# Expert sums split in two: thirteen blocks summed and stored while the last seven run, the last seven added to the output by accumulating DMAs

## What is computed

```python
x = hidden_states.reshape(-1, D)                      # 1024 tokens x 256
router_logits = x @ w_gate.T                          # 8 experts
routing_weights = softmax(router_logits)
routing_weights, selected_experts = top_k(routing_weights, 2)
routing_weights = routing_weights / sum(routing_weights)
out = zeros_like(x)
for e in range(8):
    expert_weight = sum(routing_weights * (selected_experts == e), axis=-1)
    h = silu(x @ w1[e].T) * (x @ w3[e].T)             # 704 wide
    out = out + h @ w2[e].T * expert_weight
x = x + out
```

## Time and profile before

| | |
|---|---|
| median of three runs | 648.27 us |
| the profiled execution's own time | 646.59 us |
| its span, first to last instruction | 644.8 us |
| PE busy | 506.1 us, 78% of the span |
| DVE busy | 420.6 us, 65% |
| ACT busy | 367.4 us, 57% |
| POOL busy | 150.1 us, 23% |
| first gather of the expert stage | 461.63 us |
| last result copied by ACT | 627.84 us |
| first load of `ypair` issued | 630.54 us |
| last store to `out` issued | 641.37 us |

### The profile page before, as it was taken

The page is one execution under the profiler, slowest core; times in us unless marked ns, Lnnn a source line. Parts: engine busy times, 40 slices in busy tenths (PEclk is TensorE's granted clock), DMA queues, the critical chain, the costliest instruction groups (busy, mean ns, idle before and its releaser), DMA issues.

```text
span 644.8 us, 14042 instructions
## 1 busy us (share of the span) xinstructions
PE 506.1 (78%) x5716; PEld 371.9 (58%) x5716; DVE 420.6 (65%) x632; ACT 367.4 (57%) x793; POOL 150.1 (23%) x115
## 2 busy tenths in 40 slices
PE   0287788786778855579979999986399999999980
PEld 0154555564556722354655665676399999995560
DVE  7989999999995578979986677668411111111214
ACT  7996899887888227648578657672312222221212
POOL 1000000000020228602229766410202222222110
PEclk9995699897977989799999999996699999999995
DMA  8700000000010000000000000001699999888816
GB/s 332 231 1 1 1 2 1 2 1 1 2 34 2 1 1 1 1 1 2 2 3 4 3 2 3 4 4 34 206 420 418 420 390 326 330 326 326 340 39 204
DMA packets 18336, 71.19 MB, mean 110 GB/s; under 512 B 4832, under 2 KB 9696, under 8 KB 14688
## 3 DMA queue, kind: packets, MB, share of 16 engines
q1 hardware_dynamic: 15120, 64.00, 26.2%
q0 software_dynamic: 1920, 5.25, 2.2%
q10 hardware_dynamic: 1232, 1.06, 0.5%
HBM read 65.57 MB, written 4.72 MB: 109 GB/s over the span
## 4 chain that ended last, share of the span: by engine, by line
PE 44%; DVE 40%; ACT 8%; issue 4%; DMA 2%; POOL 1%; DVEq 0%; POOLq 0%; ACTq 0%
PE PS L1522 29%; DVE arena L975 5%; DVE arena L968 4%; DVE nmx L1071 4%; DVE arena L1236 4%; PE PS L2055 2%; PE PS L1857 2%; PE PS L2124 2%; PE PS L1874 1%; DVE R L997 1%; DVE arena L990 1%; DVE arena L995 1%; DVE arena L994 1%; DVE arena L989 1%; DVE arena L987 1%
## 5 line engine op out<-in xcount | busy, mean ns | idle before, releaser
L1522 PE MATMUL PS<-arena 128*128 128x128 f32 (+5 forms) x1360 | 147.2, 286 | 16.6 <-DVE arena L1171 11.5
L1522 PEld LDWEIGHTS PS<-arena 128*128 128x128 f32 (+3 forms) x1360 | 122.8, 163 | 40.4 <-issue 23.7
L622 ACT ACTIVATE arena<-PS,nmx 128x128 f32<-128x128 f32 (+1 forms) x128 | 52.4, 433 | 21.6 <-DVE nmx L1071 21.5
L1470 DVE TENSOR_TENSOR R<-arena,PS 128x128 f32<-128x128 f32 x16 | 4.6, 288 | 89.0 <-ACT arena L885 89.0
L1587 PE MATMUL PS<-arena 32*128 32x128 f32 (+1 forms) x128 | 23.0, 440 | 32.3 <-ACT arena L622 32.3
L489 POOL DMA_INDIRECT ypair<-arena,oid x20 | 19.8, 988 | 122.3 <-ACT arena L891 122.3
L393 POOL TENSOR_SCALAR arena<-ident,gcol 128x128 f32<-128x128 f32 x4 | 3.7, 934 | 185.3 <-DMA gcol<-in_gcol 185.3
L1522 PE MATMUL PS<-arena,R 128*128 128x256 f32 x192 | 44.2, 380 | 0.6 <-ACT arena L891 0.6
L455 POOL TENSOR_TENSOR arena<-arena 128x1024 f32<-128x1024 f32 x16 | 37.6, 2372 | 21.6 <-DVE arena L1284 21.6
L1522 PEld LDWEIGHTS PS<-arena,R 128*128 128x128 f32 x192 | 35.2, 190 | 5.1 <-issue 1.0
L975 DVE TENSOR_TENSOR_SCAN arena<-dmat,arena 128x1023 f32<-128x1023 f32 x16 | 37.6, 2348 | 0.6
(11 more groups left out here) (319 smaller groups left out, 1170.2 us busy)
## 6 DMA issues: line engine op xcount, KB each, us to landing
arena<-in_moe SPq DMA_DIRECT2D x23, 1408.0 KB, 7.1
arena<-in_moe SPq DMA_DIRECT2D x23, 768.0 KB, 9.2
inproj<-in_inproj SPq DMA_DIRECT2D x1, 1344.0 KB, 10.5
arena<-in_fT SPq DMA_DIRECT2D x2, 512.0 KB, 4.2
R<-in_w1T SPq DMA_DIRECT2D x1, 1024.0 KB, 6.7
R<-in_w2T SPq DMA_DIRECT2D x1, 1024.0 KB, 8.7
R<-in_w3T SPq DMA_DIRECT2D x1, 1024.0 KB, 10.7
xT<-in_xT SPq DMA_DIRECT2D x1, 1024.0 KB, 12.7
```

The lines of the kernel that those rows point to most:

```text
L622: sc.activation(pr[u % 2][:, j, 0:n], PS[:, 2 * (u % 2) + j // 2, (j % 2) * 256:(j % 2) * 256 + n], ACT.Exp, bias=nmx[:, u % 2, j:j + 1], ...
L1522: last = mm(dst, l, r, start=(n == 0), stop=(n == len(pairs) - 1))
```

## The change

The order of the blocks becomes 0 to 8 (whole), 16, 17, 18 (two), 19 (one), 9 to 15 (whole). So the last LATE = 7 steps, 13 to 19, are whole blocks, in each of which a token occurs at most once.

- The rows of steps 0 to 12 go to `ypair` as before. SP then loads all of `ypair` (eight loads of 256 KB, all on SP's queue), behind its last load of weights. DVE sums them into `xtok`, two multiply-adds per row tile, in the middle of its work on the late steps: three quarters after `hidden_block(15)`, the last after `hidden_block(16)`. SP stores each quarter to `out`.
- Rows of `ypair` that only late steps would write must be zero. So SP fills the 2048 rows from a zero tile at the start, and also 896 new rows behind the 1024 of `out`, where padding rows of late steps go. The caller takes the first 1024 rows of the output tensor.
- In steps 13 to 19 ACT multiplies the rows by their weights as it copies them out of PSUM. These weights lie by token, not by row of a block. So `wt` is stored to a new DRAM table `wtab` (after SP's sixth set of weights), and POOL gathers one float per partition for each late block, in the turns of steps 3 to 9.
- POOL adds each late block's rows to `out` by an indirect DMA that accumulates (`compute_op=ALU.add`). Each waits for the block's result, for all four stores to `out`, and for the accumulating DMA before it. POOL's gathers for steps 17 to 19 are issued ahead of the first of these.
- DVE computes the indices of the weights and of the output rows (`late_rows`, eight instructions of 128x7) before its first hidden block.
- ACT's four loads and eight multiplications of the tail and DVE's four additions go.

```diff
-STEPS = [("whole", b) for b in range(15)] + [("two", 16), ("two", 17), ("two", 18), ("one", 19), ("whole", 15)]
+STEPS = [("whole", b) for b in range(9)] + [("two", 16), ("two", 17), ("two", 18), ("one", 19)] + [("whole", b) for b in range(9, 16)]
+LATE = 7
+LATE_OF = slice(16 - LATE, 16)
...
+            sp.wait_ge(S["pool_made"], 1)
+            load(ypair[0:OUT, :].rearrange("(i p) n -> p i n", p=P), zero[:].unsqueeze(1).broadcast_to([P, OUT // P, D]), "route")
+            load(out[N:N + LATE * P, :].rearrange("(i p) n -> p i n", p=P), zero[:].unsqueeze(1).broadcast_to([P, LATE, D]), "route")
...
-
-            sp.wait_ge(st_y, 16 * BLK)
+                if n == RING - 1:
+                    sp.wait_ge(S["act_xtok"], 3)
+                    sp.dma_start(wtab.rearrange("(p w) n -> p (w n)", p=P), wt[:].rearrange("p s i -> p (s i)")).then_inc(st_row, 16)
+
+            sp.wait_ge(st_y, 16 * (BLK - LATE))
             for q in range(4):
-                sp.dma_start(y01[:, 0, 2 * q:2 * q + 2, :], rows_of(0, q)).then_inc(ld_y[q], 16)
+                for s in range(2):
+                    sp.dma_start(y01[:, s, 2 * q:2 * q + 2, :], rows_of(s, q)).then_inc(ld_y[q], 16)
             for i in range(0, NT, 2):
                 sp.wait_ge(S["dve_out"], i // 2 + 1)
                 sp.dma_start(out[P * i:P * (i + 2), :].rearrange("(i p) n -> p i n", p=P), xtok[:, i:i + 2, :])\
                     .then_inc(st_out, 16)
             sp.wait_ge(st_out, 16 * NT // 2)
+            sp.wait_ge(st_y, 16 * BLK)
...
-            for s in range(BLK):
+            pool.wait_ge(ld["route"], 9 * 16)
+            for s in range(BLK - LATE):
                 b = STEPS[s][1]
                 pool.wait_ge(S["act_y"], s + 1)
                 pool.indirect_dma_start(ypair, bass.IndirectOffsetOnAxis(ap=oid[:, b:b + 1], axis=0),
                                         yb[s % YB], None).then_inc(st_y, 16)
                 if s + XR < BLK:
                     gather(s + XR)
+                if 3 <= s < 3 + LATE:
+                    l = s - 3
+                    pool.wait_ge(st_row, 48)
+                    pool.wait_ge(S["dve_gid"], 2)
+                    pool.indirect_dma_start(wlate[:, l:l + 1], None, wtab,
+                                            bass.IndirectOffsetOnAxis(ap=wid[:, l:l + 1], axis=0)).then_inc(ld_w, 16)
+            for s in range(BLK - LATE, BLK - XR):
+                gather(s + XR)
+            for l in range(LATE):
+                s = BLK - LATE + l
+                pool.wait_ge(S["act_y"], s + 1)
+                pool.wait_ge(S["dve_gid"], 3)
+                pool.wait_ge(st_out, 16 * (NT // 2))
+                pool.wait_ge(st_y, 16 * s)
+                pool.indirect_dma_start(out, bass.IndirectOffsetOnAxis(ap=addid[:, l:l + 1], axis=0),
+                                        yb[s % YB], None, compute_op=ALU.add).then_inc(st_y, 16)
...
-                sc.activation(yb[b % YB], bank(7, 256), ACT.Copy).then_inc(S["act_y"], 1)
+                if b < BLK - LATE:
+                    sc.activation(yb[b % YB], bank(7, 256), ACT.Copy).then_inc(S["act_y"], 1)
+                else:
+                    l = b - BLK + LATE
+                    act.wait_ge(ld_w, 16 * LATE)
+                    sc.activation(yb[b % YB], bank(7, 256), ACT.Copy, scale=wlate[:, l:l + 1]).then_inc(S["act_y"], 1)
...
-            act.wait_ge(st_y, 16 * BLK)
-            for q in range(4):
-                act.dma_start(y01[:, 1, 2 * q:2 * q + 2, :], rows_of(1, q)).then_inc(ld_y[q], 16)
-            for i in range(NT):
-                if i % 2 == 0:
-                    act.wait_ge(ld_y[i // 2], 32)
-                sc.activation(yw[:, i, :], y01[:, 1, i, :], ACT.Copy, scale=wt[:, 1, i:i + 1]).then_inc(S["act_yw"], 1)
...
+            def early_sums(q):
+
+                dve.wait_ge(ld_y[q], 32)
+                for i in (2 * q, 2 * q + 1):
+                    for s in range(2):
+                        done(v.scalar_tensor_tensor(xtok[:, i, :], y01[:, s, i, :], wt[:, s, i:i + 1], xtok[:, i, :], ALU.mult, ALU.add),
+                             "dve_out" if i % 2 and s else "dve_self")
...
+            late_rows()
             for s in range(BLK):
                 if s and STEPS[s - 1][0] != "whole":
                     turned_hidden(s - 1)
                 hidden_block(s)
+                if s == BLK - LATE + 2:
+                    dve.wait_ge(S["act_xtok"], 3)
+                    for q in range(3):
+                        early_sums(q)
+                if s == BLK - LATE + 3:
+                    early_sums(3)
```

More of the change, by code:

```diff
@@ L49, with build @@
 MAGIC = 1.5 * 2.0 ** 23
-def build(nc, a, arow, ypair, out):
+def build(nc, a, arow, ypair, wtab, out):
     F = mybir.dt.float32
@@ L240, in build @@
         tokv = spent_gate[:, 512:512 + NT * 2 * NU].bitcast(BF).rearrange("p (s i h v b) -> p s i h v b", s=2, i=NT, h=2, v=2)
-        y01 = arena[:, 0:2 * NT * D].rearrange("p (s i n) -> p s i n", s=2, i=NT)
-        yw = arena[:, 2 * NT * D:3 * NT * D].rearrange("p (i n) -> p i n", i=NT)
+        y01 = R[:, 2:4].rearrange("p s c n -> p s (c n)").rearrange("p s (i n) -> p s i n", i=NT)
         uiota = sb("uiota", [P, NU])
@@ L277, in build @@
         gid = sb("gid", [P, BLK], U32)
+        zero = arena[:, 26 * K + 512:26 * K + 768]
+        addid, addreal, wid, wpart = (sb(n, [P, LATE], U32) for n in ("addid", "addreal", "wid", "wpart"))
+        over = sb("over", [P, LATE])
+        wlate = sb("wlate", [P, LATE])
         PS = ctx.enter_context(nc.psum_tensor("PS", [P, 8, HALF], F))
@@ L292, in build @@
         st_y = sem("st_y")
+        ld_w = sem("ld_w")
         st_out = sem("st_out")
@@ L300, in build @@
             pe_y act_y dve_tokv pe_ids dve_gid dve_out pe_up pe_w act_w dve_xdt dve_xw pe_s act_s act_xbd pe_t
-            act_hgt act_rs dve_dec act_decay dve_rinv pe_r act_rT dve_num act_ekq act_ekvq act_sq act_yw
+            act_hgt act_rs dve_dec act_decay dve_rinv pe_r act_rT dve_num act_ekq act_ekvq act_sq
             dve_hqt dve_iden dve_msq dve_peak pe_rows pe_ss pool_made pool_osc pool_root dve_ht pe_ht""".split()
@@ L383, in _ @@
             done = chained(pool, "pool_self")
+            done(pool.memset(zero[:], 0.0))
             pool.memset(vv[:, :, :, HD:VW], 0.0).then_inc(S["pool_made"], 1)
@@ L695, in out_rows @@
                     act.wait_ge(S["pe_ot"], i - 1)
+                else:
+                    act.wait_ge(ld["route"], 9 * 16)
                 sc.activation(otok[i % 2], bank(4, D), ACT.Copy, scale=oscale3[:, i:i + 1])\
@@ L1382, in places @@
                 h = slice(lo, hi)
-                dve.wait_ge(ld["route"], 7 * 16)
+                dve.wait_ge(ld["route"], 9 * 16)
                 dve.wait_ge(S["pe_rank"], 4 if lo else 1)
@@ L1497, in turned_hidden, with late_rows @@
                     done(v.tensor_copy(h[0:64, 640:640 + UNIT], PS[0:64, u, 5 * UNIT:6 * UNIT]), "dve_ht")
+            def late_rows():
+                rows_ = oid[:, LATE_OF]
+                done(v.tensor_scalar(wpart[:], rows_, P - 1, None, ALU.bitwise_and))
+                done(v.tensor_scalar(wid[:], rows_, 7, None, ALU.logical_shift_right))
+                done(v.tensor_scalar(wid[:], wid[:], 2 * NT - 1, None, ALU.bitwise_and))
+                done(v.scalar_tensor_tensor(wid[:], wpart[:], float(2 * NT), wid[:], ALU.mult, ALU.add), "dve_gid")
+                done(v.tensor_scalar(over[:], rows_, float(N), -float(N), ALU.is_ge, ALU.mult))
+                done(v.tensor_tensor(addreal[:], rows_, over[:], ALU.add))
+                done(v.tensor_scalar(over[:], rows_, float(OUT), -float(P * LATE_OF.start), ALU.is_ge, ALU.mult))
+                done(v.tensor_tensor(addid[:], addreal[:], over[:], ALU.add), "dve_gid")
+            def early_sums(q):
[4 more added lines that the diff above has]
+                             "dve_out" if i % 2 and s else "dve_self")
             for h in hb:
                 done(v.memset(h[64:128, 640:768], 0.0))
+            late_rows()
             for s in range(BLK):
@@ L2237, in program @@
             for n, v in arrays.items()}
-    out = nc.dram_tensor("out_0", (N, D), mybir.dt.float32, kind="ExternalOutput").ap()
+    out = nc.dram_tensor("out_0", (N + LATE * P, D), mybir.dt.float32, kind="ExternalOutput").ap()
     arow = nc.dram_tensor("arow", (N, D), mybir.dt.float32, kind="Internal").ap()
     ypair = nc.dram_tensor("ypair", (OUT + BLK * P, D), mybir.dt.float32, kind="Internal").ap()
-    build(nc, args, arow, ypair, out)
+    wtab = nc.dram_tensor("wtab", (P * 2 * NT, 1), mybir.dt.float32, kind="Internal").ap()
+    build(nc, args, arow, ypair, wtab, out)
 def kernel(**inputs):
@@ L2253 @@
     got = r.results[0]["out_0"]
-    return np.ascontiguousarray(got).reshape(B, T, D)
+    return np.ascontiguousarray(got[0:N]).reshape(B, T, D)
```

## The result

The changed kernel takes 655.21 us (median of 4 runs, 654.69 to 655.7) against 648.12 of the kernel before, a ratio of 1.0101 with a 95% interval of 1.0077 to 1.0125. It is slower by about 7 us. Forecast were 643.6, with 638.6 to 651.0 as the range.

A forecast was written before the change was run, and what follows sets the result against it. Bound by TensorE's steps plus a 17.0 us tail behind the last result. Chain start 616.6 plus seven links, 23.1, gives 639.7; plus 0.4, span 640.1 against 644.8, 4.7 less; against the median 643.6 us, range 638.6 to 651.0.

The forecast's parts named there:

- The steps: Expert stage: a whole step starts every 7.72 us wherever it stands; last result near 628.2 without stalls, 0.4 later than before.
- Set 14 and the gathers of weights: Third two step: set 14, issued about 544.7, is wanted at 552.7, the tightest set; POOL's gathers of weights cost nothing.
- The queue of weights: SP's queue: eight sets at 5.3 us each keep it busy from 553.7 to 599.5; first `ypair` quarter lands at 603.6.
- TensorE's gap: Ahead of step 16's down projection, waiting for hidden block 16: a 4.7 us stall, up to 2.2 more by the clock.
- The chain's start: Last quarter's store to `out`, issued at 613.5, lands 3.0 us later; the first accumulating DMA goes from 616.6.
- The link: One of seven serial accumulating DMAs: landing 3.2 us (bounds 2.4 to 4.4) plus 0.1, so 3.3 each, 23.1 for seven.
- hand-over: Between one accumulating DMA's landing and the next one on POOL: taken as 0.1 us per link.
- The end: After the last accumulating DMA lands at 639.7, the span closes 0.4 us later, at 640.1.
- The rival of long links: Seven accumulating DMAs: from 3.84 us of landing the chain takes back everything; at 4.4, slower at 652.0 us; chance 0.25.

## Why the prediction was wrong

The mechanism was the one forecast: a full queue of weights, a gap on TensorE in the place named, and a chain of seven serial DMAs that ends last. The price of a link in that chain was not, and with it the sign. The forecast end of the span was 640.1, the measured one 652.7.

- **The steps**: forecast step 15 at 585.7, measured 586.08. The order alone costs nothing. Right.
- **Set 14 and the gathers of weights**: the up projection of the third two step began on time (553.11, and in the run of the order alone 552.56; forecast 552.7), and the only gap of over 1 us in the changed kernel between 480 and 606 is the one of 1.3 us that was there before. Right, cost nothing.
- **The queue of weights**: set 22 was forecast to land at 602.3; its second load was issued at 587.50 and landed 16.8 later, 604.3. The first quarter came at 605.82 instead of 603.6. Right in kind, 2.2 us short. The full queue moved 409 to 417 GB/s between 563 and 603, where 424 were reckoned; by estimate that makes about 1 us of it, and the rest is open.
- **TensorE's gap**: 6.8 instead of 4.7, and 2.2 more by the clock, as bounded: the down projection behind it took 4.94, another 2.76 at full clock. The last result came at 637.75 instead of 632.9 to 635.1. As argued, it did not set the end; taking the gap away brought nothing. The windows of the gap's end and of that down projection have the granted clock, 0.50, in the third column from the right:

```profile
612.00:613.60 1.60, 0.01 (x1) 0.01 (x1) 1.46 (x5) 0.00 (x0) 0.00 (x0) 0.50 0.31 108
613.60:615.00 1.40, 1.40 (x3) 1.16 (x4) 1.33 (x3) 0.00 (x0) 0.00 (x0) 0.50 0.19 64
```

- **The chain's start**: 618.71 instead of 616.6. The sums ended at 615.63 instead of 613.2, 2.4 late by the queue of weights. The last store was issued right behind them and had landed by 617.79, 2.2 later, where 3.3 were reckoned. And 0.9 passed from there to POOL's issue, which the forecast had at nothing in this place. That the start was only 2.1 off is partly luck, since two of these errors nearly cancel. TensorE's gap has no part in it.
- **The link**: this is the step that failed. "With 0.1 for the hand-over a link is 3.3, seven are 23.1": from first issue to last landing it was 31.8, 8.7 more. 4.7 of it is landing (27.1 in all for seven, instead of 22.4), 4.0 is hand-over (4.7 for six instead of 0.7 for seven). The landing of 3.8 lay inside the bounds of 2.4 and 4.4; I had taken the lower half on the argument that two reads overlap. For the hand-over I had put 0.1 without a row, and no bounds; it measured 0.78. The kernel before had no POOL scatter that waits for another DMA, only ones that wait for ACT, 0.28 behind it. Even that row is nearly three times the 0.1.
- **The end**: 0.4 forecast, 2.2 measured, POOL's drain. Before, the last thing was SP's store, and the drain lay beside it.

2.1, 8.7 and 1.8 are the 12.6 us. The rival of long links had the right sign and nearly the size (652.0 us at a landing of 4.4), but with its threshold at 3.84 us of landing it would have called the measured 3.8 a draw. With the hand-over of 0.78 and the drain of 2.2 the break-even lies at (644.8 - 2.2 - 618.7 + 0.78) / 7 - 0.78 = 2.7 us of landing, an estimate from these traces, only 0.3 above a plain scatter. The run of plain scatters bears it out: at 2.4 it was level with the kernel before (0.9997). So seven links in series could not have paid measurably at any landing that these runs show. The range of 638.6 to 651.0 had bounds for one term and none for the hand-over and the drain.

The rule of the Trainium skill ("DMA: Bandwidth & Descriptors", Anatomy of one DMA), from which an estimate of 2.6 us per accumulating DMA came, holds for the plain scatter (2.3 against 2.4) and not for the accumulating one, which took 3.8. That the addition itself is free ("Collectives: The Full Stack", on SDMA + CCE) is no guide to a short DMA's landing either: here the addition and its second read together cost 1.4 us each, and no run parts the two.

## What to carry to other kernels

A series of dependent DMAs costs its number times landing plus hand-over. Weigh that product, with the hand-over and the drain at the end in it, against the room that is left behind its earliest start, and choose the number of links from the two slopes; here four and not seven. Taking away the most visible gap of the busiest engine can bring nothing while such a chain runs beside it, so try the chain's length and its start first.

## What the runs showed of the hardware

- **An accumulating indirect DMA** of 128 rows of 1 KB in DRAM lands in 3.8 us (3.6 to 4.2 in the runs with a series) and takes POOL 1.56 us to issue; a plain scatter of the same rows takes 2.4 and 0.97.
- **A POOL DMA that waits for the POOL DMA before it** goes out some 0.8 us behind that one's landing, with addition or without, and 0.9 behind the landing of SP's last store. Behind the end of another POOL DMA's issue, without such a wait, it takes 0.3.
- **POOL's drain** ends 1.8 to 2.5 us behind the landing of its last DMA, and where nothing else runs longer it holds up the end of the program.
- **Issuing while the DMA engines are full blocks the issuing engine.** Eight loads of 256 KB took SP 15.85 us to issue behind the weights, and ACT 12.31 on a queue of its own, beside the weights, so another queue was no way round. With the weights done, eight took SP 3.97 (LATE = 5):

```profile
604.04 3.97 SPq L386 DMA_DIRECT2D R<-ypair  x8
```

What exactly fills up was not tried.
